# A causal-attention stage rebuilt: weight slices loaded ahead, the norm's squares on ScalarE, softmax denominators handled four query blocks at a time

## What is computed

```python
q = _l2norm(heads(Wq, bq)); k = _l2norm(heads(Wk, bk)); v = heads(Wv, bv)
scores = jnp.einsum('bhqd,bhkd->bhqk', q, k) * SCALE
scores = jnp.where(causal, -10000.0, clip(scores, -5, 5))
attn = jax.nn.softmax(scores / TEMP, axis=-1)
out = jnp.einsum('bhqk,bhkd->bhqd', attn, v)
```

## Time and profile before

| | |
|---|---|
| runs of the kernel before | 9354.49 and 9841.99 us, median 9598.24 us |
| profiled execution, own time | 9337.52 us |
| its span, first to last instruction, slowest core | 9336.0 us |
| spans of the 8 cores | 9289.7 to 9336.0 us |
| busy, whole span | TensorE matmul 54%, VectorE 23%, ScalarE 17%, GpSimd 1% |
| stretch of the attention stage | about 7031 to 9192 us from the span's start |
| in it: ScalarE table loads (L1900, L2036, L2093, L2123) | 128 + 64 + 64 + 64 |

### The profile page before, as it was taken

One profiled execution on the slowest core, in us unless ns is written; L12 is line 12 of the kernel. 1 busy time (PEld: TensorE's weight loads), 2 busy tenths in 40 slices (PEclk: granted clock), 3 DMA queues, 4 the chain that ended last, 5 costly groups with the idle time before them and its releaser, 6 DMA issues.

```text
span 9336.0 us, 61248 instructions; the slowest of 8 cores (9289.7 to 9336.0 us)
## 1 busy us (share of the span) xinstructions
PE 5056.5 (54%) x21376; PEld 2204.8 (24%) x21376; DVE 2140.4 (23%) x4180; ACT 1608.5 (17%) x2110; POOL 77.9 (1%) x154
## 2 busy tenths in 40 slices
PE   0007445676554799899982255555542434435355
PEld 0003222232222344344431122222211111111111
DVE  2110011111111122222236635000003223231323
ACT  0012100000000011011003020000011533526252
POOL 0000000000000000000000000000000000000000
PEclk9999777888777899999996578777765655556567
DMA  9999999999999800100011001555510000000001
GB/s 124 125 129 120 128 127 122 124 121 124 126 128 125 116 28 28 46 36 28 28 37 36 18 11 45 206 198 205 201 56 5 3 5 3 3 5 0 5 3 63
DMA packets 172911, 709.40 MB, mean 76 GB/s; under 512 B 9974, under 2 KB 22262, under 8 KB 162698
## 3 DMA queue, kind: packets, MB, share of 16 engines
q0 software_dynamic: 14720, 325.86, 29.6%
q1 hardware_dynamic: 157898, 379.62, 12.5%
HBM read 1014.51 MB, written 341.84 MB: 145 GB/s over the span
## 4 chain that ended last, share of the span: by engine, by line
PE 49%; DMA 14%; another core or an unknown queue 11%; DVE 9%; ACT 8%; issue 4%; DVEq 2%; ACTq 1%; SPq 0%; PEldq 0%; POOL 0%; POOLq 0%
PE p_pg L520 11%; PE p_pu L529 11%; PE p_pd L589 11%; DMA p1b<-x_in 3%; DMA p1a<-x_in 3%; PE p_pqk L1861 3%; PE p_pav L2072 3%; DMA p_wch<-wu1B 2%; PE p_psc L2017 2%; PE p_pe L1641 2%; DMA p_wch<-wg1B 2%; ACT L1900 2%; PE p_pg L1525 1%; ACT p_exps L2036 1%
## 5 line engine op out<-in xcount | busy, mean ns | idle before, releaser
L520 PE MATMUL p_pg<-fmbuf,wg_s 128*128 128x512 bf16 x4608 | 1117.7, 386 | 1159.3 <-DMA wu_s<-wuB 934.3
L529 PE MATMUL p_pu<-fmbuf,wu_s 128*128 128x512 bf16 x4608 | 1098.4, 381 | 0.0
L562 DVE TENSOR_TENSOR h_b<-p_sl,p_pu 128x512 bf16<-128x512 bf16 x576 | 395.8, 687 | 2839.5 <-PE p_pu L529 2255.5
L589 PE MATMUL p_pd<-wd_s,h_b 128*128 128x512 bf16 x4608 | 997.4, 379 | 20.0 <-DVE h_b L562 20.0
L520 PEld LDWEIGHTS p_pg<-fmbuf,wg_s 128*128 128x128 bf16 x4608 | 455.2, 99 | 1724.0 <-issue 1197.3
L552 ACT ACTIVATE p_sl<-p_pg 128x512 bf16<-128x512 f32 x576 | 344.1, 597 | 1580.2 <-PE p_pg L520 1580.0
L529 PEld LDWEIGHTS p_pu<-fmbuf,wu_s 128*128 128x128 bf16 x4608 | 454.3, 99 | 555.9 <-issue 21.7
L589 PEld LDWEIGHTS p_pd<-wd_s,h_b 128*128 128x128 bf16 x4608 | 449.6, 98 | 567.8 <-issue 28.4
L617 DVE SCALAR_TENSOR_TENSOR xacc<-p_pd,cw_cols,xacc 128x1024 f32<-128x1024 f32 x256 | 328.6, 1284 | 584.3 <-PE p_pd L589 584.3
L330 PE MATMUL fb_p<-ident_b,fb_tm 128*128 128x128 bf16 x384 | 48.5, 306 | 729.6 <-DVE fb_tm L313 657.6
L2017 PE MATMUL p_psc<-Qf,Kf 64*128 64x512 bf16 x640 | 301.2, 606 | 236.5 <-ACT p_prds L2123 125.9
(11 more groups left out here) (230 smaller groups left out, 3709.8 us busy)
## 6 DMA issues: line engine op xcount, KB each, us to landing
wg1B<-wg POOLq DMA_DIRECT2D x16, 4096.0 KB, 41.1
wu1B<-wu POOLq DMA_DIRECT2D x16, 4096.0 KB, 41.4
wd1B<-wd POOLq DMA_DIRECT2D x16, 4096.0 KB, 41.3
p_wch<-wg1B SPq DMA_DIRECT2D x32, 2048.0 KB, 11.8
p_wch<-wu1B SPq DMA_DIRECT2D x32, 2048.0 KB, 10.3
p_wch<-wd1B SPq DMA_DIRECT2D x64, 1024.0 KB, 7.3
wgB<-wgT POOLq DMA_DIRECT2D x8, 4096.0 KB, 41.1
wuB<-wuT POOLq DMA_DIRECT2D x8, 4096.0 KB, 41.1
```

Of the source, the lines that this page charges most:

```text
L520: ins = tn.matmul(pg[p][:], wg_s[:, c * 1024 + ic * 128: c * 1024 + ic * 128 + 128], fmbuf[:, c * TOK + n * 512: c * TOK + n * 512 + 512], ...
L529: ins = tn.matmul(pu[p][:], wu_s[:, c * 1024 + ic * 128: c * 1024 + ic * 128 + 128], fmbuf[:, c * TOK + n * 512: c * TOK + n * 512 + 512], ...
L562: ins = v.tensor_mul(h_b[:, ic * TOK + n * 512: ic * TOK + n * 512 + 512], tsil[p][:], pu[p][:])
L589: ins = tn.matmul(pd[p][:, nn * 512:(nn + 1) * 512], h_b[:, ic * TOK + t * 128: ic * TOK + t * 128 + 128], wd_s[:, ic * 1024 + nn * 512: i ...
```

## The change

It rewrites the attention stage only.

- All SBUF tiles of the stage are allocated once, outside the `hq` loop. `wsl` keeps two buffers, and the load of a slice waits only for the last reader of its own buffer (`wsl_last`), where there was one.
- The bias is no longer broadcast once a pass and added by VectorE; a matmul of one row (`ones_row` by the bias row) opens each tile's accumulation.
- The squares and their sums move to ScalarE, as four activations with an accumulator output in a closure of their own (`fsA`); VectorE keeps the lower bound (`fvmx`), and `fvq2` reads PSUM. The small buffers go from two to four.
- `fvv` copies straight from PSUM.
- `psc` becomes 128x512, one key tile each, and exp is taken of 128x512 at a time.
- `pav` has four tiles, and the denominators of a head's four blocks are handled together after the last one.

```diff
+                wsl_last = {}
...
+                wsl = [sbuf(f"p7_w{i}", [128, NCH * 256], BF16, p7)
+                       for i in range(2)]
+                brow2 = [sbuf(f"p7_brb{i}", [1, 256], BF16, p7)
...
-                            sy.wait_ge(T.h, t_emit)
-                            if hq + which == 0:
+                            if wfree is not None:
+                                sy.wait_ge(T.h, wfree)
+                            else:
+                                sy.wait_ge(T.h, te)
                                 sy.wait_ge(V.h, tv)
                                 sy.wait_ge(S.h, ts)
...
-                            ins = tn.matmul(pbb[:], ones_row[:], brow_b[:],
-                                            start=True, stop=True)
...
+                                    if which == 0 and ao_prev is not None:
+                                        tn.wait_ge(V.h, ao_prev)
+                                        tn.wait_ge(S.h, srd_prev)
+                                if wt >= 4 and (wt - 4) in pq_free:
+                                    tn.wait_ge(V.h, pq_free[wt - 4])
+                                tn.matmul(pqk[q][:], ones_row[:],
+                                          brow2[wq_][:],
+                                          start=True, stop=False)
...
-                                    v.tensor_add(q32[:], pqk[q], bcb[:])
-                                    v.drain()
-                                    v.tensor_mul(qsq[:], q32[:], q32[:])
-                                    v.drain()
+                                def fsA(sc, q=q, ttok=ttok,
+                                        rn_prev=rn_done.get(wt - 4)):
+                                    sc.wait_ge(T.h, ttok)
...
                                     for hh in range(4):
-                                        v.reduce_sum(
-                                            ssq2[q2][:, hh:hh + 1],
+                                        ins = sc.activation(
                                             qsq[:, hh * 64:(hh + 1) * 64],
-                                            axis=AX)
+                                            pqk[q][:, hh * 64:(hh + 1) * 64],
+                                            ACT.Square,
+                                            accum_out=ssq4[q][:, hh:hh + 1])
+                                    S.inc(ins)
+                                block.scalar(fsA)
+                                def fvmx(v, q=q, sa_tok=sa_tok):
+                                    v.wait_ge(S.h, sa_tok)
                                     ins = v.tensor_scalar_max(
...
-                                            q32[:, hh * 64:(hh + 1) * 64],
-                                            rn82[q2][:, hh:hh + 1], None,
+                                            pqk[q][:, hh * 64:(hh + 1) * 64],
+                                            rn84[q][:, hh:hh + 1], None,
...
-                                    v.tensor_add(q32[:], pqk[q], bcb[:])
-                                    v.drain()
...
-                                        dst, q32[:].rearrange(
+                                        dst, pqk[q][:].rearrange(
...
+                        wsl_last[which % 2] = T.n
...
-                        psc = [psum(f"p7_psc{i}", [128, 1024], F32, pa)
+                        psc = [psum(f"p7_psc{i}", [128, 512], F32, pa)
                                for i in range(2)]
                         pav = [psum(f"p7_pav{i}", [128, 512], F32, pa)
-                               for i in range(2)]
+                               for i in range(4)]
...
+                                        pp = kt % 2
+                                        if kt >= 2:
+                                            tn.wait_ge(S.h, s0 + kt - 1)
+                                        elif gidx > 0 or hq > 0:
+                                            tn.wait_ge(S.h, s0)
...
+                                    for kt in range(nk):
+                                        sc.wait_ge(T.h, t0 + kt + 1)
                                         ins = sc.activation(
+                                            exp_sb[:, kt * 512:
+                                                   (kt + 1) * 512],
+                                            psc[kt % 2][:], ACT.Exp)
                                         S.inc(ins)
...
+                            def fvdB(v, av3=av_tok[3], sd_prev=sd_last):
+                                v.wait_ge(T.h, av3)
...
+                                for js in range(4):
+                                    ins = v.tensor_copy(
+                                        dn4[0:1, js * 512:(js + 1) * 512],
+                                        pav[js][64:65, :])
...
+                            def fsdB(sc, dn_tok=dn_tok):
+                                sc.wait_ge(V.h, dn_tok)
+                                sc.activation(dn4[:], dn4[:], ACT.Ln)
+                                sc.drain()
+                                ins = sc.activation(dn4[:], dn4[:],
+                                                    ACT.Exp, scale=-1.0)
...
+                            def fvd2B(v, rd_tok=rd_tok):
+                                v.wait_ge(S.h, rd_tok)
+                                ins = v.tensor_copy(rd4[:], dn4[:])
...
+                            for js in range(4):
+                                def ftrd(tn, js=js, rdb_tok=rdb_tok,
+                                         srd_prev=srd_last):
                                     tn.wait_ge(V.h, rdb_tok)
+                                    if srd_prev is not None:
+                                        tn.wait_ge(S.h, srd_prev)
+                                    ins = tn.matmul(
+                                        prd[:], ones_row[0:1, 0:64],
+                                        rd4[0:1, js * 512:(js + 1) * 512],
...
+                                    ins = sc.copy(
+                                        prd_sb4[:, js * 512:(js + 1) * 512],
+                                        prd[:])
```

More of the change, by code:

```diff
@@ L1793, in build_core_program @@
                     qhat_rd = {}
-                    for which, (w_in, b_in, isv) in enumerate(
-                            ((wqT_in, bq_in, False), (wkT_in, bk_in, False),
-                             (wvT_in, bv_in, True))):
+                    pq_free = {}
+                    for which, (b_in, isv) in enumerate(
+                            ((bq_in, False), (bk_in, False), (bv_in, True))):
                         wq_ = which % 2
-                        t_emit = T.n
                         wB = (wqB, wkB, wvB)[which]
@@ L1817, in build_core_program, with fgwb @@
                         block.sync(fgw)
-                        def fgwb(g, hq=hq, b_in=b_in, BRL=BRL, t_emit=t_emit):
-                            g.wait_ge(T.h, t_emit)
-                            g.dma_start(out=brow_b[:],
+                        def fgwb(g, hq=hq, b_in=b_in, BRL=BRL, wq_=wq_,
+                                 te=T.n, wfree=wsl_last.get(which % 2)):
+                            if wfree is not None:
+                                g.wait_ge(T.h, wfree)
+                            else:
+                                g.wait_ge(T.h, te)
+                            g.dma_start(out=brow2[wq_][:],
                                         in_=b_in[:, hq * 256:(hq + 1) * 256]
@@ L1996, in build_core_program @@
                             ccl = h8 // 2
+                            av_tok = {}
                             for js in range(4):
@@ L2026, in fA, with fS @@
                                             start=True, stop=True)
-                                        if kt % 2 == 1 or kt == nk - 1:
-                                            T.inc(ins)
+                                        T.inc(ins)
                                 block.tensor(fA)
-                                def fS(sc, nk=nk, npair=npair, t0=t0):
-                                    for pair in range(npair):
-                                        w = 1024 if 2 * pair + 1 < nk else 512
-                                        sc.wait_ge(T.h, t0 + pair + 1)
-                                        pp = pair % 2
+                                def fS(sc, nk=nk, t0=t0):
+                                    for kt in range(nk):
+                                        sc.wait_ge(T.h, t0 + kt + 1)
                                         ins = sc.activation(
-                                            exp_sb[:, pair * 1024:
-                                                   pair * 1024 + w],
-                                            psc[pp][:, 0:w], ACT.Exp)
+                                            exp_sb[:, kt * 512:
+                                                   (kt + 1) * 512],
+                                            psc[kt % 2][:], ACT.Exp)
                                         S.inc(ins)
@@ L2091, in fsd @@
```

(30 more changed lines are left out.)

163 lines of the change are left out of this document (68 added, 95 removed).

## The result

The changed kernel takes 9435.49 us (median), the kernel before, over more runs than were shown ahead of the prediction, 9367.66. Some runs of either kernel are slower by a few per cent because the cores of one or both dies show a lower clock; without them the ratio is 1.0078, with a 95% interval of 1.0062 to 1.0094. That is 73 us slower (58 to 88), under the 2% that counts as a difference. The profiled execution took 9438.11 us with a span of 9435.9, 99.9 more than before.

The account below looks back on a forecast made before the run. Bound by handoff chains in the q and k tiles and at attention block ends, not by any engine; 9337.5 + 195 - 38 + 6 + 78 - 119 = 9460 us, range 9350 to 9560, about 8 in 10.

Parts of the forecast that it names:

- the term of the q and k tile: Q and k passes, 128 tiles: table load, squares, handoff, bias matmul and PSUM reads outweigh VectorE's saving; +1.52 each, +195 us.
- the sums: Attention, TensorE's sums in `fB` after a block's exps: no change was costed, 0 us.
- slice loads, v pass: Projection: slices loaded ahead save waits at pass boundaries, -38 us; bias matmuls lengthen four v passes, +6 us.
- exps, 640 key tiles: Attention: narrower exps keep the round trip, 0.71 us a key tile against 0.57; +78 us for 16 heads.
- denominators, 16 heads: Attention, head ends: one chain of 19.5 us replaces four of 6.74; 7.5 us less a head, -119 us.
- the rival of dear squares: Q and k tile: four squares with reads at their upper bound of 2.0 us; 9559 us, over 2% slower; chance 0.15.
- the prediction's own bound of 55: Attention exps: +55 us instead of +78 if a third of it runs at the upper clock.
- one of its signs of being wrong: Attention: the prediction called itself wrong if the scores run at the upper clock.
- The rival of a warmer TensorE: Attention: fewer pauses keep TensorE's clock at its upper level, speeding exps and sums; 9331 us, no slower; chance 0.09.
- The rival of deeper buffers: Q and k: the next tile's matmuls run inside this tile's chain; -283 us, 9177 us; chance 0.02.

Follow-up runs that it names:

- the first experiment: The changed kernel with `fsA` and `fsq` in one ScalarE closure, every operation and wait kept: ratio 0.983 to the kernel before, projection 990.0 us against 1155.8.
- wide scores: The changed kernel with score tiles 128x1024 again, `prd` sharing the first one's memory: ratio 0.996 to the kernel before, attention 984.5 us against 1085.4.

## Where the prediction failed, and what of it held

The prediction was wrong in its size: 122 us more, 9460, was forecast, and 73 were measured, with 84 in the stage. The step that failed is the term of the q and k tile, +195, which measured +140; beside it the sums, put at nothing, cost 26. The mechanism (a chain in the written order, a table load for every ScalarE closure in it) and the direction held, and the time lies in the range. By its terms:

| term | forecast | in the profiles | |
|---|---|---|---|
| q and k tile, 128 | +195 (1.52 each) | +140 (1.09) | mis-sized |
| slice loads, v pass | -38, +6 | -27 together | near |
| exps, 640 key tiles | +78 | +65 | near |
| the sums behind them | 0 | +26 | missed |
| denominators, 16 heads | -119 | -120 | held |

Some of the agreement is luck: the tile and the exps were put 68 us too dear, the sums, and the loads with the v pass, 31 too cheap, so that only 38 are left of it in the sum.

**The tile.** What failed is the price of the parts, not the chain. Four squares and reads take 0.93 us (7069.52 to 7070.45), below my 1.3 and below the lower bound of 1.0: read and next square overlap by 0.1 each way, which no row of before showed. With that the rival of dear squares (2.0) is out. The bias row costs 0.46 on this chain and not 0.30: I took the slot between a row and the next matmul and missed that the row also starts later behind the transposes than a full matmul does. And there was a gain that I hadn't looked for: in the mean of all these tiles VectorE began 0.25 us after the matmuls' end before, and ScalarE's load begins 0.16 after it now (0.24 and 0.08 in the tiles shown, 7064.92 to 7065.16 and 7068.14 to 7068.22; the matmuls' ends are modelled). With 1.28, 0.93, 0.11, 0.46 and 0.12 for the PSUM reads, less 1.68 and 0.09, the sum is 1.13; 1.09 is measured.

**The load** per closure was right, and the first experiment shows it by itself: taking the closure boundary away and nothing else gives back 1.28 us a tile. The Trainium skill's rule ("ScalarE: Activation LUTs", section on table sets) of cheap functions in every set isn't what sets the number of loads in this kernel: the copies of `fsrd` have 64 loads for 64 closures. Square, Ln and Exp do run behind one load, but only inside one closure.

**Loads ahead.** Worth 4.4 at each k and v boundary as forecast (4.6), but the v pass took back 3.5 us of it and not the 1.5 that I used, more than my upper bound of 3: from the last k transposes to the first scores it took 23.7 to 24.7 us before and 23.0 after. TensorE became the bound there, at 1.19 us a tile, and without the rows the stretch is 6.5 us shorter.

**The exps** went as worked out (1.4 us a pair of key tiles), and came out 13 us cheaper. Some of the scores ran at the upper clock (granted 0.57 over all of them, where 0.5 was assumed), as the prediction's own bound of 55 allowed for. That was also one of its signs of being wrong, and it came in part.

**The sums** are the missed term. I costed `fB` at nothing, but its granted clock fell from 0.63 to 0.57 in the mean: 26 us, of which wide scores give back 19. The rival of a warmer TensorE came true for the scores (0.51 to 0.57), had the wrong sign for the sums, and over the first group's attention as a whole the clock stayed at 0.61.

**The range's other cases.** The rival of deeper buffers was rightly ruled out by the order: in the changed kernel no matmul of the next tile runs inside a tile's chain, and with the order written for it the projection is 470 us shorter. Whether that order needs four small buffers wasn't run.

The change is thus a sum of gains and losses of which 84 us are left: the batched denominators (-120), the loads ahead (-36) and the addition on VectorE that went, with the quicker squares and start that came with it (-98, by difference), against squares in a closure of their own (+165 in the kernel before), bias rows (+81) and narrow scores with their slower sums (+91 by the table above; undoing them gave 101 back). What is worked out by difference, and the denominators, have no experiment of their own.

## What to carry to other kernels

Moving work from one engine to another gains nothing by itself where a handoff chain sets the time. Count the links, and each new ScalarE closure as a link with its own table load, and put everything that can share a closure into one. More buffers need an order that uses them: emit the next tiles' matmuls ahead of the last step of this one. When PSUM is short, look for a tile that may share another's bank before halving the one that feeds the slowest loop.

## What was not expected of the hardware

- An activation with an accumulator output is two instructions, and in a row they overlap on both sides: four of 64 columns with their reads take 0.93 us, though their durations (0.22 and 0.21) add up to 1.7.
- How soon an engine starts behind a matmul depends on the place more than on the engine: VectorE began 0.25 us after the eight matmuls of a q or k tile before, but 0.11 after the transposes.
- A one-row bias matmul is not small: 0.46 us on the chain ahead of eight matmuls that take 1.89, and leaving out all 192 took 81 us off.
- The granted clock of the sums changed with the width of the score tiles ahead of them: 0.57 with narrow and 0.61 with wide ones, 585 ns a matmul against 553, with the same number of matmuls.
